# Moving the scan tiles of the next batch among the routed bodies of a state-space and mixture-of-experts kernel

## The reference, cut to what matters

```
x = x + tanh(g_x) * ssm(ctx, layernorm(x))       # state-space scan
x = x + tanh(g_f) * moe(layernorm(x))            # 8 experts, 6 of 64 slots taken, and a shared one

state = state * dA + (d_t * u_t)[..., None] * B_t     # 512 channels x 16 states, over 512 steps
y_t   = einsum('ben,bn->be', state, C_t)
out   = x @ W.T + scale * mix(x, qa, qb, w)           # each linear map of an expert
```

## Time and profile before

| | us |
|---|---|
| median of the runs | 1644.08 |
| the profiled execution | 1648.37 |
| its span | 1646.5 |
| TensorE busy | 1539.3 (93%) |
| VectorE busy | 1160.1 (70%) |
| GpSimd busy | 732.9 (45%) |
| ScalarE busy | 656.3 (40%) |

### The profile page before, as it was taken

One profiled execution on the slowest core, in us unless ns is written; L12 is line 12 of the kernel. 1 busy time (PEld: TensorE's weight loads), 2 busy tenths in 40 slices (PEclk: granted clock), 3 DMA queues, 4 the chain that ended last, 5 costly groups with the idle time before them and its releaser, 6 DMA issues.

```text
span 1646.5 us, 19454 instructions
## 1 busy us (share of the span) xinstructions
PE 1539.3 (93%) x6728; PEld 1134.1 (69%) x6728; DVE 1160.1 (70%) x1635; ACT 656.3 (40%) x1035; POOL 732.9 (45%) x536
## 2 busy tenths in 40 slices
PE   5678699898888899999999999999999999999999
PEld 3334477666666677777777778777777777777776
DVE  6899864898999857588988755788898553333333
ACT  7555344544454433444444344434443321111111
POOL 3589310688888801167778301377787000000000
PEclk9799899999999999999999999999999999999999
DMA  7799437688888674765667445577765556466652
GB/s 260 263 331 312 179 131 250 215 287 295 273 283 290 232 271 166 256 218 203 211 235 250 173 166 189 205 270 244 257 206 178 185 191 211 165 213 209 215 188 80
DMA packets 118930, 368.60 MB, mean 224 GB/s; under 512 B 21072, under 2 KB 48720, under 8 KB 103600
## 3 DMA queue, kind: packets, MB, share of 16 engines
q1 hardware_dynamic: 109360, 333.54, 58.4%
q10 hardware_dynamic: 9472, 33.82, 6.3%
HBM read 297.78 MB, written 68.16 MB: 222 GB/s over the span
## 4 chain that ended last, share of the span: by engine, by line
PE 62%; DVE 17%; issue 6%; ACT 5%; DMA 4%; POOL 4%; SPq 1%; DVEq 0%; ACTq 0%; POOLq 0%
PE b_g L773 15%; PE b_u L773 14%; PE b_u L865 8%; DVE ring L1547 5%; PE b_q L819 4%; PE b_g L865 4%; PE b_q L865 3%; DVE ring L1553 3%; PE b_g L837 3%; PE b_g L804 2%; POOL ring L1446 2%; DMA raw<-in_gu 2%; DVE tt L1521 2%; DMA qat<-scr_qa 2%; PE b_g L797 1%
## 5 line engine op out<-in xcount | busy, mean ns | idle before, releaser
L1446 POOL TENSOR_TENSOR ring<-du,rep 128x512 f32<-128x512 f32 x256 | 345.0, 1356 | 112.8 <-DVE du L1626 81.9
L773 PE MATMUL b_g<-xnb,gm 128*128 128x512 f32 (+1 forms) x1440 | 359.4, 398 | 1.0 <-DVE xnb L1524 0.9
L773 PE MATMUL b_u<-xnb,gm 128*128 128x512 f32 (+1 forms) x1440 | 349.9, 392 | 0.6 <-DVE xx L1521 0.6
L1455 POOL TENSOR_TENSOR yx<-yx,ring 128x512 f32<-128x512 f32 x192 | 261.8, 1363 | 128.8 <-DVE ring L1553 128.0
L773 PEld LDWEIGHTS b_g<-xnb,gm 128*128 128x128 f32 (+1 forms) x1440 | 253.1, 180 | 92.0 <-issue 27.2
L1547 DVE TENSOR_TENSOR_SCAN ring<-b_a,ring 128x512 f32<-128x512 f32 x256 | 310.7, 1214 | 5.5 <-ACT b_a L1012 3.7
L773 PEld LDWEIGHTS b_u<-xnb,gm 128*128 128x128 f32 (+1 forms) x1440 | 256.8, 179 | 73.4 <-DVE xx L1521 2.0
L1012 ACT ACTIVATE b_a<-delta,a_neg 128x512 f32<-128x512 f32 x256 | 173.2, 680 | 96.2 <-DVE ring L1547 96.2
L1521 DVE SCALAR_TENSOR_TENSOR tt<-tt,b_g 128x512 f32<-128x512 f32 (+1 forms) x120 | 82.0, 684 | 181.8 <-ACT tt L1012 181.6
L865 PE MATMUL b_u<-dwt,hhl 128*128 128x512 f32 (+1 forms) x720 | 191.1, 395 | 0.8 <-issue 0.7
L1012 ACT ACTIVATE tt<-b_g 128x512 f32<-128x512 f32 (+1 forms) x120 | 71.1, 593 | 266.2 <-PE b_u L804 235.3
(11 more groups left out here) (249 smaller groups left out, 2076.5 us busy)
## 6 DMA issues: line engine op xcount, KB each, us to landing
gm<-scr_gm SPq DMA_DIRECT2D x64, 1024.0 KB, 9.1
dwt<-scr_dw SPq DMA_DIRECT2D x32, 1536.0 KB, 6.6
rep<-bc_d ACTq DMA_DIRECT2D x64, 512.0 KB, 6.8
gm<-scr_gm SPq DMA_DIRECT2D x32, 768.0 KB, 4.6
scr_gm<-gm SPq DMA_DIRECT2D x20, 1024.0 KB, 7.9
dqt<-scr_dq SPq DMA_DIRECT2D x25, 640.0 KB, 8.4
qat<-scr_qa SPq DMA_DIRECT2D x25, 512.0 KB, 9.8
raw<-in_gu SPq DMA_DIRECT2D x16, 704.0 KB, 8.2
```

What stands on the lines that cost most here:

```text
L773: i = mm(out_b[0:IW[m], :], w, v, start=(n == 0), stop=(n == 11 and not is_routed(s)))
L1446: v.tensor_tensor(ring_at(nb, T), du[:, T % 4, :], rep[:, N % NREP, 0], ALU.mult).then_inc(pool_dbu, 1)
L1455: v.tensor_tensor(yd, yd, ring[:, T % NRING], ALU.add).then_inc(pool_y, 1)
```

## The change

Batches 0, 1 and 2 get another table of tiles. Body e0 held 4 tiles (one each in d and e, two in f) and has 7 now (one each in c, h2 and e, two each in d and f). Bodies e1 to e3 keep 10. Bodies e4 to e6 had 10 and have 9: slot a holds one tile in place of two. As 7 is no multiple of 4, the copies of C come to stand in other slots too. GpSimd's loop takes the number of tiles of a body from the same table. One wait is new, in the prologue.

```diff
         def first_tile(e):
-            return 0 if e == 0 else 4 + 10 * (e - 1)
+            return (0, 7, 17, 27, 37, 46, 55)[e]

         def tiles_in(e, slot):
             t0 = first_tile(e)
             if e == 0:
-                return {"d": (0,), "e": (1,), "f": (2, 3)}.get(slot, ())
-            return {"a": (t0, t0 + 1), "h0": (t0 + 2,), "b": (t0 + 3,), "h1": (t0 + 4,), "c": (t0 + 5,),
+                return {"c": (0,), "h2": (1,), "d": (2, 3), "e": (4,), "f": (5, 6)}.get(slot, ())
+            if e > 3:
+                t0 -= 1
+            return {"a": (t0, t0 + 1) if e <= 3 else (t0 + 1,), "h0": (t0 + 2,), "b": (t0 + 3,), "h1": (t0 + 4,), "c": (t0 + 5,),
                     "h2": (t0 + 6,), "d": (t0 + 7,), "e": (t0 + 8,), "f": (t0 + 9,)}[slot]
...
             def state_rows(nb):
                 act.wait_ge(pe_xd, nb + 1)
+                if nb == 0:
+                    act.wait_ge(act_gw, 3)
                 rounded(s_r, ba[0][:]).then_inc(act_sr, 1)
```

## The result

The changed kernel took 1657.47 us, the median of 4 runs (1654.56 to 1659.17), the kernel before 1644.01 (1643.23 to 1644.24). The ratio is 1.0081, with a 95% interval of 1.0063 to 1.0098: 13.5 us slower, where 3.6 were forecast and 1653 was the range's end. Measured again on another chip, in the first experiment, it was 1.0076 (1.0064 to 1.0089), or 11.6 us between the medians. So the sign was right and the size was off by 8 to 10 us.

The account below looks back on a forecast made before the run. TensorE was taken to bound batches 1 and 2, VectorE with the weight splitting batch 0. Batches 1 and 2 summed to +6.5 us and batch 0 to -2.9: +3.6 on 1644.08 gave 1647.7, range 1640 to 1653.

Parts of the forecast that it names:

- Body e0 of batches 1 and 2, +4.0 each: Later lo and dawf make TensorE wait; the first add_down and e1's `b_u` come later: +4.0 us a batch, +8.1 together.
- load wait of e1: Batches 1 and 2: TensorE's wait in e1 for the `qat` load shrinks by 0.3 us each, together -0.6.
- Bodies e3 and e4, +0.9 and -1.4: Batches 1 and 2: moved copies of C cost e3 0.9 us; e4 loses TensorE's wait, -1.4; together +1.8 and -2.8.
- The clock: Second rival: TensorE's clock falls once in each of batches 1 and 2 behind e0's new waits, +3.4, 1651.1 us; chance 0.20.
- Bodies e4 to e6 of batch 0, -2.2, -3.5 and -0.95: One tile less in slot a and fewer VectorE stalls at copies of C shorten these bodies by these us.
- GpSimd's shift: Batch 0, e0: splitting of `gm` falls some 4 us later, covered by the longer body; otherwise up to 2 us a body.
- The prediction's own sign of being wrong: Wrong if e0 of batch 2 stays under 37 us, copies in a and c cause no VectorE wait, or batch 0 is off by over 4.
- Body e0 of batch 0, +4.2, with e1, +1.05: VectorE's path: e0's add_down comes 4.2 us later; in e1 the copy moved to a's second tile adds 1.05.
- Bodies e2 and e3: Batch 0: e2 loses the copies of h0 and h2, -2.56 us; e3 gains 1.05 from the copy in a.
- The first: Rival: copies in a and c cost nothing, as the tanh behind them waits for TensorE's chunk; 1639.9 us; chance 0.17.
- The third: Rival: loads hold batch 0, so e4 and e5 give back only half of 2.2 + 3.5; 1650.6 us; chance 0.11.
- The fourth: Rival: half of the new waits in e0 don't show, half of 8.1 goes; 1643.7 us, no change; chance 0.12.

Follow-up runs that it names:

- the first experiment: The changed kernel run once more, unaltered, on another chip: 1656.3 us, ratio 1.0076 against the kernel before.
- the third experiment: New table in batches 1 and 2 only, batch 0 keeping the old one: 1655.2 us, ratio 1.0063 against the kernel before.
- The second experiment: New table in batch 0 only, batches 1 and 2 keeping the old one: 1647.7 us, ratio 1.0018 against the kernel before.
- The fifth experiment: New table in batch 0 only, GpSimd's weight splitting and scaling one tile step earlier in e4 to e6: 1645.2 us, ratio 0.9996 against the kernel before.
- the extra products: Changed kernel with six down products done twice in e0 of batches 1 and 2, ahead of the wait for dawf: 1654.3 us, ratio 1.0057 against the kernel before.
- The extra products in batch 0: Six down products done twice in e1, e2, e4, e5, e6: new table in batch 0 only, 1646.2 us (1.0004); kernel before, 1644.9 us (0.9994).
- both edits together: New table in batch 0 only, GpSimd's steps one earlier in e4 to e6, six products twice in five bodies: 1644.0 us, ratio 0.9987 against the kernel before.

## Why the prediction was wrong, step by step

**Body e0 of batches 1 and 2, +4.0 each: right, and in part by luck.** With the clock up, e0 and e1 together grew by 3.7 (70.8 to 74.5), and the sum had 4.0 less 0.3. The waits are those named, 1.72 for chunk 2 where 1.8 was worked out, and 2.3 to 2.4 for dawf where it was 1.8, with 0.7 of it from the `awp` beside GpSimd; the two other steps that the prediction weighed beside GpSimd, the lo (0.68) and daw_s (0.70), lost nothing. Against these 4.1 the whole load wait of e1 went, 1.2 us in batch 2 before, where -0.3 was the term, and TensorE's busy time grew by 0.8 with the same instructions, which no term had.

**Bodies e3 and e4, +0.9 and -1.4: right.** Bodies e2 to e4 shrank by 0.8 a batch, the sum had -0.5.

**The clock: the step that failed in batches 1 and 2.** It stood among the rivals, at +3.4 and a chance of 0.20, because a wait of 1.32 us had left the clock alone. It fell in 6 of 8 such bodies, at 2.1 us each in the pair of bodies (76.6 against 74.5). The sum had nothing for it. Without falls the part is 2 x (3.7 - 0.8) = 5.8, with 1.5 falls 9.0; the third experiment measured 10.4, in an interval of 8.4 to 12.5. A wait of 1.82 with a fall behind it was in the earlier trace rows, and that was the nearer row to a wait of 1.8.

**Bodies e4 to e6 of batch 0, -2.2, -3.5 and -0.95: the step that failed in batch 0.** The second experiment shows the windows (e4 and e5, then e6):

```profile
450.60:533.60 83.00, 74.94 (x317) 54.51 (x317) 74.91 (x82) 42.19 (x64) 72.84 (x48) 0.94 0.87 293
533.60:576.60 43.00, 39.16 (x159) 28.94 (x160) 34.03 (x39) 17.38 (x27) 32.09 (x22) 0.88 0.64 227
```

Against 84.7 and 39.4 before, they give -1.7 and +3.6 where -5.7 and -0.95 were forecast. Single profiles scatter: over the four of the new table and the three of the old one without other edits in batch 0, the means differ by -1.6 and +2.4 (and those of e7 behind them by -1.1). In e4 and e5 VectorE's work fell by 3.5 us (78.45 to 74.91), the two tiles, but its idle time rose by 1.8, where the sum had it fall by more than 2. In e6 its work is the same and its idle time rose by 3.7. The stalls at the copies that should go went in part (VectorE's waits for the rounding of a lo in e4 to e6: 6.4 to 3.8 us); others came in their place: for the tanh (2.4 to 5.9), for qbt (0.9 to 3.5) and for TensorE's down products (none to 2.0). ScalarE's tanh itself waited longer for TensorE, before and in the second experiment:

```profile
ACT tt L1012 <- PE b_u L804: 2.0, 1, 2.0
```

```profile
ACT tt L1023 <- PE b_u L815: 7.6, 3, 3.1
```

So the step that failed is that the sum followed VectorE's own path and let what it won come off the body. The fifth experiment shortens e4 and e5 by 1.8 us (83.0 to 81.2) by GpSimd's steps, and e6 goes with the clock. I wrote that GpSimd's shift would be covered in e0 and did not follow it into the bodies of nine tiles, where the loop counts steps from the table that the change had shortened. The prediction's own sign of being wrong, a batch 0 off by more than 4, came true: it was off by 5.8.

**Body e0 of batch 0, +4.2, with e1, +1.05: near.** The pair went from 85.3 to 89.9 us in the first profile after, +4.6 where 5.25 was the sum. The copies in the second tile of a and in c cost what was said (2.62 and 1.29). Bodies e2 and e3 lost 1.7 together (85.9 to 84.2), where -1.5 was the sum.

**The rivals.** The first, that these copies cost nothing, is refuted by those two rows of e1; its reason, a tanh that waits for TensorE anyway, holds in e4 to e6, above. The third, loads, holds in part. ScalarE's waits for the raw weights in e4 to e6 (us, times, longest), before and in the second experiment:

```profile
ACT gm L1012 <- DMA raw<-in_gu: 2.9, 2, 1.8
```

```profile
ACT gm L1023 <- DMA raw<-in_gu: 5.2, 3, 2.7
```

The load came no earlier. In e6 ScalarE waited 2.7 us for it, with the exp and the tanh of chunk 2 next in its order, and VectorE stood and waited for that tanh:

```profile
553.76 0.68 DVE L1534 SCALAR_TENSOR_TENSOR tt<-tt,b_g 96x512 f32<-96x512 f32 x1 [1.57 <-ACT tt L1023]
```

The fourth is refuted by the waits in e0. The second is shown by the twelve products (4.58 against 3.00) and the whole batches (355.8 against 353.5), and the extra products take it away.

What stays open: why the clock fell behind one wait of 2.3 us and not behind another, and how the 5.8 us that batch 0 missed divide among TensorE's products, the clock, the loads and qbt; whether GpSimd's steps would have sped up the kernel before as well; the longer e6 at a lower clock is read from profiles, not from a run that changes the clock in e6 alone. The extra products in batch 0 moved the time by an amount that its interval hardly tells from nothing; only both edits together are clear of it.

## What to carry to other kernels

When a table of work is shifted, look for every loop that counts in the same units, also on engines that wait for nothing: here GpSimd's step numbers stayed those of ten tiles a body, and one step less for the bodies of nine was worth about 3 us. A new wait on a busy TensorE should be charged twice, for itself and for a clock that may fall behind it; some cheap products that are thrown away show which of the two it is. And a wait that is taken away from one step of a chain comes back at the next: the sum must go to the end of the body, and past VectorE to the engine that it then waits for.

## What the runs showed of the hardware

- Products that nobody needs made a kernel faster: in e0, 1.36 us of them in a wait of 2.3 us kept the granted clock at full in 4 of 4 profiled bodies (it fell in 6 of 8 without them), and the time fell from a ratio of 1.0076 to 1.0057, with intervals that just overlap.
- One and the same VectorE subtraction of two SBUF tiles (`qat`, 128 x 512) took 0.68 to 2.90 us, by what GpSimd did beside it: 2.90 in e4 of the second experiment, behind an operation of GpSimd that had begun first, 0.68 in e4 of the fifth.
- A profiled execution stood 4.3 us above the median before and 2.9 below it after; with several falls of the clock in each execution, two profiles gave less than half of the measured difference.
